# Flamingo block on one core: the eight experts' weight loads move from SyncE's queue to ScalarE's, behind the last values

## The reference

```
x = x + tanh(g_xattn[0]) * attention_16_heads_of_16(layernorm(x), ctx)        # 375 context rows
x = x + tanh(g_ffn[0])   * moe_linear_top2_of_8(layernorm(x))
x = x + tanh(g_xattn[1]) * perceiver_attention_16_heads_of_64(ctx, layernorm(x))   # 487 keys
x = x + tanh(g_ffn[1])   * moe_swiglu_top2_of_8(layernorm(x))   # W1 256 -> 2*512, W2 512 -> 256
```

## Time and profile before

| | |
|---|---|
| median of 3 runs | 1386.96 us |
| profiled execution | 1387.11 us, its span 1385.3 us |
| busy share PE / DVE / ACT / POOL | 88% / 77% / 72% / 59% |
| mean granted TensorE clock | 0.946 |

### The profile page before, as it was taken

How to read it: one execution, slowest core, us unless ns; L and a number is a source line. 1 busy time by engine, 2 the same in 40 slices (tenths; PEclk the granted TensorE clock), 3 DMA queues, 4 the chain that set the end, 5 groups by cost and what they waited for, 6 DMA issues and landing times. The chain is left out here.

```text
span 1385.3 us, 38079 instructions
## 1 busy us (share of the span) xinstructions
PE 1223.9 (88%) x13060; PEld 876.8 (63%) x13060; DVE 1073.1 (77%) x3112; ACT 996.9 (72%) x2552; POOL 813.8 (59%) x1204
## 2 busy tenths in 40 slices
PE   5999999999985499999999999999999985299994
PEld 3777777777774245566656566656566654299994
DVE  4899999999995268888888888888888873377772
ACT  3888888888883368887787887877887872166662
POOL 3544555455433346777777777777777663255664
PEclk8899999999997699999999999999999996599997
DMA  6545455444320149787788777888778797833323
GB/s 173 162 135 155 148 146 168 122 131 148 100 60 13 47 98 163 138 149 145 152 159 161 142 149 143 154 161 162 139 147 140 152 224 148 328 64 60 60 37 76
DMA packets 309406, 185.50 MB, mean 134 GB/s; under 512 B 257930, under 2 KB 295186, under 8 KB 306112
## 3 DMA queue, kind: packets, MB, share of 16 engines
q1 hardware_dynamic: 293024, 140.82, 47.6%
q0 software_dynamic: 13168, 35.80, 10.6%
q10 hardware_dynamic: 3024, 6.47, 1.6%
HBM read 76.19 MB, written 49.94 MB: 91 GB/s over the span
## 5 line engine op out<-in xcount | busy, mean ns | idle before, releaser
L1716 ACT ACTIVATE b_prob<-b_prob,b_top 112x487 f32<-112x487 f32 x256 | 178.9, 699 | 30.7 <-DVE b_top L1842 29.1
L1349 POOL TENSOR_TENSOR w_pool<-b_prob,w_pool 112x487 f16<-112x487 f32 x128 | 147.0, 1149 | 86.6 <-ACT w_pool L1741 85.2
L1527 PE MATMUL b_ps_p<-w_s,b_tok_s 128*128 128x512 f16 (+1 forms) x768 | 187.7, 381 | 4.0 <-DVE w_pool L1829 3.3
L1527 PE MATMUL b_ps_p<-b_tok_s,w_s 128*128 128x487 f16 x768 | 182.9, 376 | 6.5 <-POOL b_tok_s L1343 3.7
L1842 DVE CUSTOM_DVE_ANT_0 b_prob<-b_ps_s,b_keep 112x487 f32<-112x487 f32 x256 | 167.3, 654 | 23.9 <-PE b_ps_s L1620 22.3
L739 ACT ACTIVATE w_pool<-w_pool,a_top 112x375 f32<-112x375 f32 x256 | 155.1, 606 | 5.0 <-DVE a_top L874 2.0
L1741 ACT ACTIVATE w_pool<-b_prob 112x487 f16<-112x487 f32 x256 | 155.9, 609 | 0.4
L874 DVE CUSTOM_DVE_ANT_0 w_pool<-a_ps_s,a_keep 112x375 f32<-112x375 f32 x256 | 137.7, 538 | 13.1 <-PE a_ps_s L632 13.0
L1635 PEld LDWEIGHTS b_ps_o<-w_pool 128*128 128x128 f16 (+1 forms) x3072 | 123.8, 99 | 36.3 <-DMA w_pool<-w_pool 16.4
L1635 PE MATMUL b_ps_o<-w_pool 128*128 128x64 f16 (+1 forms) x3072 | 134.8, 195 | 13.3 <-DMA w_pool<-w_pool 13.3
L640 PE MATMUL a_ps_t<-a_const,w_pool 112*125 112x112 f32 x768 | 135.4, 286 | 11.3 <-ACT w_pool L739 8.8
(11 more groups left out here) (261 smaller groups left out, 2967.8 us busy)
## 6 DMA issues: line engine op xcount, KB each, us to landing
xs<-w_pool SPq DMA_DIRECT2D x14, 1032.0 KB, 4.2
w_pool<-w_split SPq DMA_DIRECT2D x8, 1600.0 KB, 12.2
b_wch_f<-in_w_experts POOLq DMA_DIRECT2D x32, 384.0 KB, 5.2
w_split<-b_wch_s POOLq DMA_DIRECT2D x32, 384.0 KB, 3.4
w_pool<-keys SPq DMA_DIRECT2D x96, 93.8 KB, 3.2
a_ctx_f<-in_ctxT SPq DMA_DIRECT2D x16, 375.0 KB, 3.9
keys<-a_k_s SPq DMA_DIRECT2D x16, 375.0 KB, 3.0
b_ctx_t<-in_ctx SPq DMA_DIRECT2D x16, 375.0 KB
```

The source lines that it names most:

```text
L1349: pool.tensor_tensor(halves[:, h % TURN, LO, 0:NK], prob[:, h % RING, 0:NK], halves[:, h % TURN, HI, 0:NK], ALU.subtract).then_inc(s_lo[1], 1)
L1527: last = pe.matmul(out, sta(a, k), mov(m, k), start=(k == 0 and n == 0), stop=(k == tiles - 1 and n == 2))
L1716: act.activation(prob[:, h % RING, 0:NK], prob[:, h % RING, 0:NK], ACT.Exp, bias=top[:, h % RING:h % RING + 1], scale=-1.0, accum_out=sums ...
```

## The change

All eight loads are taken off SP's program, including the two in the last batch, and stand in ACT's, behind its copy of the second half of `oT` of the last batch (`hitem(B - 1, 1)`, L1709). ACT waits for the values of the last batch and for the chunk stores once, before the first. SP's wait for the last store goes from the end of the second phase; the semaphore (now `s_acc`, made outside the phase) is waited for by POOL in the third phase, before its first addition of rows.

```diff
@@ sync, second phase
-            def load_expert(e):
-                need(sp, s_pv, H, B - 2 if e < 2 else B - 1, H)
-                if e >= 2:
-                    for j in range(2):
-                        sp.wait_ge(s_wchstore[j], 16 * B)
-                sp.dma_start(w_pool[:, e, :], w_dram[e]).then_inc(s_w[e], 16)
-
             def body(b, par):
                 for s in range(H):
-                    if not ahead(b, 1) and s in (7, 9):
-                        load_expert((s - 7) // 2)
...
             residual(B - 1)
             store(B - 1)
-            for e in range(2, E):
-                load_expert(e)
-            sp.wait_ge(s_store, 16 * B)
@@ scalar, second phase
+            def load_expert(e):
+                if e == 0:
+                    need(act, s_pv, H, B - 1, H)
+                    for j in range(2):
+                        act.wait_ge(s_wchstore[j], 16 * B)
+                act.dma_start(w_pool[:, e, :], w_dram[e]).then_inc(s_w[e], 16)
...
             for k in range(HI_):
                 hitem(B - 1, k)
+                if k == H_O - 1:
+                    for e in range(E):
+                        load_expert(e)
             weigh(B - 1)
@@ gpsimd, third phase
             def add_rows(i):
+                if i == 0:
+                    pool.wait_ge(s_acc, 16 * B)
                 pool.wait_ge(s_yout, i + 1)
```

More of the change, by code:

```diff
@@ L1031, in phase_attention_large_heads @@
                                 x2_dram, acc_dram, xs_dram, w_all, w_dram, b2_all, ones, cum, s_rows, head, s_head,
-                                ident_h, s_ident, b1_f, w_pool, s_w):
+                                ident_h, s_ident, b1_f, w_pool, s_w, s_acc):
     with ExitStack() as ctx:
@@ L1168, in phase_attention_large_heads @@
         s_ratio = sem("ratio")
-        s_store = sem("store")
         s_const2 = sem("const2")
@@ L1251, in store @@
                 need(sp, s_hfree, HI_, c, H_O + 1, settled)
-                sp.dma_start(acc_dram[bass.ds(c * T, T), :], x3[:, :]).then_inc(s_store, 16)
+                sp.dma_start(acc_dram[bass.ds(c * T, T), :], x3[:, :]).then_inc(s_acc, 16)
             def turn(b, h):
@@ L1866, in hitem @@
                     need(dve, s_rload, 16, c, 16)
-                    need(dve, s_store, 16, c, 0)
+                    need(dve, s_acc, 16, c, 0)
                     dve.scalar_tensor_tensor(x3[:, :], ps_x[0:T, 0:D], tanhs[0:T, 1:2], x_res[:, :], ALU.mult, ALU.add).then_inc(s_hfree, 1)
@@ L1967, with phase_experts @@
 TABLE_COUNT, TABLE_ROW = 4, 18
-def phase_experts(nc, w_dram, xs_dram, acc_dram, ones, cum, s_rows, head, s_head, ident, s_ident, b1_f, w_pool, s_w, out):
+def phase_experts(nc, w_dram, xs_dram, acc_dram, ones, cum, s_rows, head, s_head, ident, s_ident, b1_f, w_pool, s_w, s_acc, out):
     with ExitStack() as ctx:
@@ L2312, in build_program @@
         w_pool = ctx.enter_context(nc.sbuf_tensor("w_pool", [128, E, SW], F16))
+        s_acc = ctx.enter_context(nc.semaphore("acc_store"))
         s_w = [ctx.enter_context(nc.semaphore(f"w{e}")) for e in range(E)]
@@ L2319, in build_program @@
                                         a["b2"], a["wr1"], a["br1"], a["consts"], w1_s, x2, acc, xs, a["w_experts"],
-                                        w_split, a["b2_experts"], ones, cum, s_rows, head, s_head, ident_h, s_ident, b1_f, w_pool, s_w)
-        phase_experts(nc, w_split, xs, acc, ones, cum, s_rows, head, s_head, ident_h, s_ident, b1_f, w_pool, s_w, out)
+                                        w_split, a["b2_experts"], ones, cum, s_rows, head, s_head, ident_h, s_ident, b1_f, w_pool, s_w, s_acc)
+        phase_experts(nc, w_split, xs, acc, ones, cum, s_rows, head, s_head, ident_h, s_ident, b1_f, w_pool, s_w, s_acc, out)
 def kernel(x, ctx_1024, mask_BxSxS2_ff1, mask_BxS2_bk0, g_xattn, g_ffn,
```

## The result

| | median us | lowest to highest | runs |
|---|---|---|---|
| before | 1387.64 | 1385.55 to 1389.78 | 10 |
| after | 1384.78 | 1382.58 to 1387.87 | 10 |

The ratio is 0.9975, with a 95% interval of 0.9965 to 0.9984. The medians differ by 2.9 us; the ratio stands for 3.5 us, its interval for 2.2 to 4.9 us. 7.8 us were forecast. The profiled execution after took 1384.93 us, its span is 1383.1 us. The forecast span was 1385.3 - 7.8 = 1377.5 us.

The account below looks back on a forecast made before the run. Bound: the string of row additions, moving as one block with the third phase's start, set by the barrier's opening and first rows' landing. Terms 7.8 + 0 + 0 + 0: 1387.1 - 7.8 = 1379.3 us; range 1375.0 to 1385.5 us.

Parts of the forecast that it names:

- Last batch: Last batch of the second phase: without the two loads between them, turns land sooner; 7.8 us gained, ends 7.0 and 8.7.
- head 7's by POOL: Last batch: head 7's turn waits for POOL's low half, ended near 1142.7 us, and lands at 1145.6 us.
- Serial piece: From the last values to the last indirect DMA: same instructions, ACT's 4.3 us of load issues covered by 5 us; 0.
- Loads' end and drain: At the barrier: loads end at 1196.7 us, still costing POOL's drain some 4 to 5 us as now; 0.
- First rows: Start of third phase: first tile's rows land as now; 0, from 1.5 us gained to 0.8 us later.
- held until the big load is through: Upper bound for the first rows' load: held back by the weight load, it lands 0.5 to 0.8 us later.
- The wait for the last store: SP's wait ended 5.4 us before POOL's drain began; moved to the first addition, it has some 12 us cover; 0.
- It and the copy to the output move as one block: Third phase: the string of row additions, one each 4.5 us, moves unchanged with the phase's start.
- the first: Rival, smaller gain: only the first PE wait in the last batch is the loads' doing; 1383.9 us, chance 0.15.
- The second: Rival, larger gain: upper clock into the product with Wout (2.5 us), first rows free (up to 1.5); 1376.8 us, chance 0.12.
- The third: Rival, slower: ACT's loads hold back POOL's queue until the last expert lands at 1196.7 us; 1399 us, chance 0.09.
- The fourth: Rival, no change: loads don't hold up the last batch, or the gain is lost at the drain; 1387 us, chance 0.08.

Follow-up runs that it names:

- before_tiny01: Kernel before, with the two weight loads in the last batch cut to 16 of 6400 columns each; 1385.54 us, ratio 0.9963.
- one_load: Kernel after, with seven of the eight weight loads cut to 16 columns and all stage copies reading expert 0; 1375.54 us in one run.
- sp_same_place: Kernel after, with the eight loads issued by SP between the residual and the last store instead of by ACT; 1384.12 us, ratio 0.9959.
- sp_deferred: Kernel after, with loads 0 to 2 on SP between residual and last store, 3 to 7 on ACT in the third phase; 1387.47 us, ratio 0.9990.
- tiny_copies: Kernel after, with DVE's weight copies to the stage cut to 16 columns from the fifth tile on; 1384.79 us, ratio 0.9960.

## Why the prediction was right and wrong

The direction was right and the median lies in the range, 0.7 us below its upper end; the size was wrong: 2.9 us for 7.8 us. That the range held it is partly luck, since it was wide enough for a rival with another mechanism.

- **Last batch, 7.8 us (ends 7.0 and 8.7): mis-sized, it measured 5.9 us.** The mechanism was right: before_tiny01 has the whole of it from the two loads' bytes. Up to head 5 the times came as worked out (values from 1142.24 us: 1141.43 and 1142.85; scores of 12 and 13 at 1143.3: 1143.30, in 0.82 us as the upper clock level gives). The step that failed first is "head 7's by POOL, whose first of two low halves ... ends near 1142.7 us": POOL was busy with a chunk's split until 1142.16 us, so the turn went out at 1143.72 us and PE waited 1.93 us. The two low halves stood at 1141.42 us in the earlier trace rows, and I had left POOL's other work where it stood. The last scores then start 6.5 us earlier than before, where 8.1 us were worked out. The rest went behind them: head 14's maxima start 6.5 us earlier (1155.72 to 1149.25 us), head 15's 6.0 us (1158.03 to 1152.01 us), head 15's turn 5.3 us (1162.06 to 1156.73 us) in this pair of traces. I had the maxima that rows 7 call the last as head 15's and had not counted what DVE does between the two. What holds the turn for the last 0.7 us wasn't followed up.
- **Serial piece, 0: right.** From the last turn to the barrier 32.9 us before and 32.8 us after. ACT's 4.5 us of issues ended 4.7 us before its next copy.
- **Loads' end and drain, 0: right in sum, the end 3 us off.** 1199.8 us for 1196.7. The loads start 2.3 us later than forecast (1164.44 us for 1162.1), since the last batch gave less, and the eight take 35.3 us for 34.6. The drain was 8.3 us for 8.1, and one_load prices the loads in it at 4.2 us, as estimated.
- **First rows, 0 (-1.5 to +0.8): wrong, beyond the upper end.** 1.5 us longer to land, 1.0 us at y0. The forecast took 7.8 us off both the loads' end and the rows' issue. Measured from T0, the issue moved 5.9 us and the loads' end 4.4 us, which is the 1.5 us: in all fourteen traces in which the weight loads still ran at the issue, the rows landed 0.25 to 0.4 us behind the last weight load. So of the two bounds of the forecast the upper one, "held until the big load is through", is what the traces show; sp_same_place, with the loads over, needs 2.1 us.
- **The wait for the last store, 0: right.** It landed 8.1 us after 1170.75 us, 33.7 us ahead of the first addition (1212.51 us); no kernel shows POOL waiting for it.
- **"It and the copy to the output move as one block": wrong.** The string of additions is only 0.06 us a tile slower than the compute beside it, the two meet, and the phase is longer by what they lose there: 1.8 us on the means. With two strings the block does move whole, 4.5 us by the times and 4.9 us in the traces. I read "one each 4.5 us" as a fixed rate of the DMA, and did not ask what one tile of compute takes.

The terms as measured: 5.9 - 1.0 - 1.8 = 3.1 us. Of the rivals, the first came nearest by its number (3.25 us) but not by its mechanism, since the second wait did shrink, from 4.24 us to 0.40 and 1.93 us. The second fell: the product with Wout took 4.49 us, not 2.83, and the rows came later. The third, POOL held back until the last expert lands, fell: `rows(B-1)` started at 1172.87 us, 0.5 us behind DVE's `xn3`. The fourth fell by the interval.

## What to carry to other kernels

When the chain of waits is one long string of equal steps, compare its step with the step of the compute beside it before you move it as a block: here 4.55 against 4.49 us, and a gain ahead of it came through by 3.1 of 4.9 us. Place big loads by the small transfers that meet them, not only by their own consumers: 1600 KB loads in flight cost 4 to 5 us at a drain behind indirect DMAs, 7 us at the second addition of sp_deferred, and up to 3 us at a load of rows; issued 4.8 us earlier, or partly behind the barrier, they cost less. Where idle time of one engine goes, redo the queues of all others in that stretch, their unrelated work too.

## What the runs showed of the hardware

- POOL's drain at a barrier, with an indirect DMA of a batch's rows just issued, took 4.1 to 4.5 us with few or no loads left and 8.0 to 9.1 us beside the queue of loads.
- A load of one tile's rows landed in 2.0 to 2.2 us with no weight load beside it. Where weight loads still ran at its issue it took 2.5 to 5.3 us and landed 0.25 to 0.4 us behind the last of them, whether they stood in its own queue (before) or in ACT's (after).
- DVE's copy of 128x1600 f16 takes 0.56 us. Beside POOL's low half it took 1.48 us and ended 0.45 us after POOL's did (1286.05 against 1285.60 us), and POOL's issue of an indirect DMA grew from 1.55 to 2.07 us beside such copies. DVE's copy of 128x8 f32, 0.17 us beside a tile of after, took 2.48 us beside POOL's issue and low half and ended 0.04 us after them (1245.42 against 1245.38 us, tiny_copies). The Trainium skill, "SBUF — State Buffer", section "SBUF: two separate sides", calls the port pair of the two engines an exclusive lock held for a whole instruction; the ends of the two copies just behind POOL's work fit that.
